# DLRM interaction tower on one core: ScalarE's copies of the first half's gram no longer stand behind the weight transfers

## The reference

```python
e = jnp.stack([tbl_0[ids[:, 0]], ..., tbl_26[ids[:, 26]]], axis=1)      # (2048, 27, 128)
interactions = jnp.einsum('bfd,bgd->bfg', e, e).reshape(B, F * F)
z = jnp.concatenate([r_bottom_mlp_out, interactions[:, TRIL_IDX]], axis=1)
h = jnp.concatenate([z, r_bottom_mlp_out], axis=1)                        # (2048, 607)
h = jnp.maximum(h @ W_top1 + b_top1, 0.0)                                 # 512
h = jnp.maximum(h @ W_top2 + b_top2, 0.0)                                 # 256
y = h @ W_top3                                                            # 1
```

## Time and profile before

| | |
|---|---|
| plain runs, median of 3 | 412.73 us (412.5 to 413.49) |
| profiled execution, span from first to last instruction | 563.8 us |
| mean granted TensorE clock in it | 0.845 |
| TensorE busy | 395.0 us (70% of the span) |
| POOL busy | 292.0 us (52%) |
| VectorE busy | 231.8 us (41%) |
| ScalarE busy | 156.7 us (28%) |
| DMA, mean | 72 GB/s |

### The profile page before, as it was taken

How to read it: one execution, slowest core, us unless ns; L and a number is a source line. 1 busy time by engine, 2 the same in 40 slices (tenths; PEclk the granted TensorE clock), 3 DMA queues, 4 the chain that set the end, 5 groups by cost and what they waited for, 6 DMA issues and landing times.

```text
span 563.8 us, 9147 instructions
## 1 busy us (share of the span) xinstructions
PE 395.0 (70%) x3669; PEld 336.8 (60%) x3669; DVE 231.8 (41%) x430; ACT 156.7 (28%) x337; POOL 292.0 (52%) x284
## 2 busy tenths in 40 slices
PE   1620868397979578688939587797979490924987
PEld 1520756285868467576737376676857390823977
DVE  3530667073836143373617052472716050422430
ACT  3200543021424142324115042322215041401433
POOL 6776007656574747374735737373746656172010
PEclk9975898688989979699969879697979785885999
DMA  8761272122331312041411212140413111030000
GB/s 212 193 170 47 79 185 70 48 84 66 93 86 29 99 35 74 23 118 34 145 28 62 76 33 72 24 117 24 131 37 75 48 53 51 6 95 19 16 8 9
DMA packets 20737, 40.50 MB, mean 72 GB/s; under 512 B 7128, under 2 KB 11428, under 8 KB 20696
## 3 DMA queue, kind: packets, MB, share of 16 engines
q1 hardware_dynamic: 11674, 21.64, 14.1%
q0 software_dynamic: 8960, 18.22, 12.8%
q10 hardware_dynamic: 62, 0.06, 0.1%
HBM read 36.81 MB, written 0.01 MB: 65 GB/s over the span
## 4 chain that ended last, share of the span: by engine, by line
PE 51%; issue 18%; another core or an unknown queue 11%; DVE 8%; DVEq 3%; ACT 3%; DMA 3%; SPq 1%; ACTq 0%
PE col_bank L687 17%; PE gram_bank L723 15%; PE mlp_bank L778 6%; PE mlp_bank L746 6%; DVE mask L583 4%; PE col_bank L706 4%; DVEq L590 3%; PE mlp_bank L742 2%; DMA b<-in_b 2%; DVE mask L587 2%; ACT eT L438 1%; DMA pairs<-in_tbl 1%; DVE parts L624 1%; DVE eT L608 1%
## 5 line engine op out<-in xcount | busy, mean ns | idle before, releaser
L311 POOL DMA_INDIRECT rows<-in_tbl,idx x272 | 285.5, 1050 | 219.2 <-PE gram_bank L723 138.1
L687 PE MATMUL col_bank<-mask,parts 125*128 125x512 f32 (+3 forms) x768 | 168.0, 381 | 21.8 <-DVE parts L624 12.2
L687 PEld LDWEIGHTS col_bank<-mask,parts 125*128 125x128 f32 x768 | 139.8, 204 | 45.0 <-DVE parts L624 12.1
L583 DVE TENSOR_SCALAR mask<-hot_i,rowid 125x1024 fp32r<-125x1024 int32 (+3 forms) x152 | 103.9, 684 | 65.0 <-remote 30.6
L723 PE MATMUL gram_bank<-eT 128*58 128x52 f32 x2048 | 87.2, 244 | 59.6 <-issue 54.0
L723 PEld LDWEIGHTS gram_bank<-eT 128*58 128x58 f32 x2048 | 78.5, 160 | 71.3 <-issue 67.1
L618 DVE COPY pairs<-gram_bank 26x208 f32<-26x208 f32 x128 | 46.7, 365 | 159.4 <-remote 91.5
L706 PE MATMUL col_bank<-ident,rows 128*128 128x128 f32 x272 | 41.7, 293 | 82.5 <-issue 30.5
L468 ACT ACTIVATE pairs<-gram_bank 26x208 f32<-26x208 f32 x128 | 44.5, 348 | 153.0 <-remote 84.6
L706 PEld LDWEIGHTS col_bank<-ident,rows 128*128 128x128 f32 x272 | 32.4, 149 | 90.7 <-issue 88.4
L424 ACT ACTIVATE eH<-col_bank 128x512 f32<-128x512 f32 (+3 forms) x30 | 15.3, 516 | 148.4 <-issue 59.6
(11 more groups left out here) (34 smaller groups left out, 83.9 us busy)
## 6 DMA issues: line engine op xcount, KB each, us to landing
hot_i<-in_hot_ids SPq DMA_DIRECT2D x13, 512.0 KB
rows<-in_tbl,idx POOLq DMA_INDIRECT x272
pairs<-in_tbl SPq DMA_DIRECT2D x8, 448.0 KB
hot_i<-in_hot_ids SPq DMA_DIRECT2D x8, 256.0 KB
pairs<-in_tbl SPq DMA_DIRECT2D x2, 560.0 KB
bottom<-in_bottom SPq DMA_DIRECT2D x8, 128.0 KB
hot_i<-in_hot_ids SPq DMA_DIRECT2D x2, 384.0 KB
x<-pairs SPq DMA_DIRECT2D x16, 39.0 KB
```

The lines of the kernel that those rows point to most:

```text
L311: pool.indirect_dma_start(out=rows_of(h, g)[:, i * D:(i + 1) * D], out_offset=None, in_=tables[GATHERED_TABLES[f]], in_offset=bass.Indirec ...
L583: last = nc.vector.tensor_scalar(mask[0:ROWS, entry % MASKS, 0:2 * size], ids, row_of(ks[0], c), None, ALU.is_equal)
L687: last = nc.tensor.matmul(col_bank[fill % BANKS][:, 0:size], parts[k][0:ROWS, part, c * D:(c + 1) * D], mask[0:ROWS, entry % MASKS, at:at ...
```

## The change

ScalarE's wait for the nine weight transfers, between placing half 0 in `eT` and copying half 0's gram, is left out. Nothing is put elsewhere; VectorE's and TensorE's own waits for the weights stay.

```diff
@@ -516,7 +516,6 @@
                         act.wait_ge(col_copied[fill % BANKS], fill // BANKS + 1)
                 last = place_hot(0, m)
             last.then_inc(hot_copied, 1)
-            act.wait_ge(weights_loaded, 16 * WEIGHT_LOADS)
 
             copy_pairs(0)
             place_early(1)
```

## The result

The changed kernel takes 411.67 us (median of 20 runs) where the kernel before takes 412.81 (20 runs): ratio 0.9965, with a 95% interval of 0.9949 to 0.9981. So it is faster by 1.4 to 2.4 us, and not by the 5.2 us that were forecast.

A forecast was written before the change was run, and what follows sets the result against it. It took a plain run as mostly TensorE's work, with TensorE or POOL the bound later. Stop 3.3 + set 0.9 + lookup 2.0 = 6.2 us, or 4.2 if POOL; middle 5.2, so 407.5 us, range 404.0 to 412.8.

The forecast's parts named there:

- The wait and the stop: Half 0's gram: without ScalarE's 5.44 us wait for the last bias, TensorE no longer stops before the fourth set, 3.27 us less.
- the upper bound: Front of a plain run: gathers beside the weights put them back by about 2.4 us, so the gain could reach 8.6 us.
- The clock: TensorE behind the stop: full clock returns 0.9 us in the fourth gram set and 2.0 us in the lookup.
- The rule taken from the Trainium skill: TensorE: after waiting long enough for a transfer it is throttled and restarts at half rate; with it 6.2 us, without 3.3.
- VectorE's masks: Lookup behind half 0's gram: masks at 0.765 us each keep up with TensorE's 0.94 us per entry.
- a sign of being wrong: Half 0 or 1: the forecast is wrong if TensorE stops at another place for as long.
- All three come 4.2 us earlier: End of half 0's fourth gram set: SyncE's x transfers, POOL's half 2 gathers and TensorE's lookup start 4.2 us earlier.
- Either may be: Halves behind half 0's gram: TensorE or POOL may be the bound, gaining up to 6.2 or 4.2 us; middle 5.2 taken.
- A: Half 0's gram: in a plain run the weights are in time and ScalarE never waits; 412.7 us, no change; chance 0.11.
- B: Half 1's copies: x stands in line behind the weights, so asking 4.2 us earlier brings nothing; 412.7 us; chance 0.04.
- C: Half 1's copies: x lands late beside weights and ids, TensorE stops at the fourth set; 417.9 us; chance 0.05.
- The 10.35 us of the earlier trace: Half 1's copies: their wait until 108.81 us in the profile ahead of the prediction, used for B and to price C.

The follow-up runs named there:

- base_d: The kernel before, unchanged, run again for an undisturbed profile; 413.69 us beside 413.14, ratio 0.9983.
- few_wait_c: The kernel before, with the wait, without 3 of the 17 gathers of each half from half 2 on; 395.89 us, ratio 0.9564.
- delay16_b: The changed kernel with 16 unneeded copies on ScalarE where the wait stood; ratio 1.0034 to the kernel before.
- delay32: The changed kernel with 32 unneeded copies on ScalarE where the wait stood; ratio 1.0271 to the kernel before.
- delay8_b: The changed kernel with 5.3 us of unneeded copies on ScalarE where the wait stood, second run; 410.3 us, ratio 0.9918 to the kernel before.
- after_c: The changed kernel itself, run again on one chip with a delayed version; 411.3 us, ratio 0.9941 to the kernel before.
- The doses: The changed kernel with 8, 16 or 32 unneeded copies on ScalarE where the wait stood; ratios 0.9921, 1.0034 and 1.0271 to the kernel before.
- few_nowait_c: The changed kernel without 3 of the 17 gathers of each half from half 2 on; 388.66 us, ratio 0.9399 to the kernel before.
- base_again: The kernel before, unchanged, run again for a second profile at a disturbed time; 551.5 us beside 550.5.
- delay8: The changed kernel with 8 unneeded copies on ScalarE where the wait stood; ratio 0.9921 to the kernel before.

## Why the prediction was wrong

**The wait and the stop.** Right in kind, and low in size: 3.27 us forecast, 4.07 measured in base_d and 5.97 in few_wait_c. The bias landed 18.5 us after the last table's request in base_d and not 16.7. There the gathers run beside the weights, as the upper bound had it with 2.4 us; that they are the reason was not tested.

**The clock.** The fourth set takes 1.06 us in place of 1.40, and the lookup 7.55 in place of 8.77, the very 7.55 of the earlier trace rows. The granted clock in the kernel before (base_d) and in the changed one, stretch by stretch:

```profile
56.00:57.00 1.00, 0.87 (x26) 0.87 (x28) 0.00 (x0) 0.94 (x4) 0.76 (x1) 0.84 0.33 87
57.00:58.00 1.00, 1.00 (x13) 0.86 (x10) 0.41 (x2) 0.93 (x4) 0.18 (x1) 0.50 0.13 33
58.00:62.00 4.00, 4.00 (x15) 3.16 (x14) 3.50 (x6) 1.76 (x4) 3.09 (x2) 0.74 0.19 47
```

```profile
52.00:54.00 2.00, 2.00 (x10) 1.64 (x9) 1.89 (x4) 1.61 (x4) 1.73 (x1) 1.00 0.76 216
54.00:58.00 4.00, 4.00 (x20) 3.30 (x19) 3.27 (x5) 0.00 (x0) 3.08 (x4) 1.00 0.40 119
...
62.00:66.00 4.00, 3.44 (x15) 3.06 (x15) 2.56 (x5) 1.93 (x4) 3.08 (x4) 0.50 0.21 60
```

So 0.3 + 1.2 us came back where 0.9 + 2.0 were forecast: the clock fell later, inside the set, and was back sooner. The rule taken from the Trainium skill ("TensorE: Matmul & The Clock Gate", HAM oscillation) agrees with this pair: with the stop of 4.07 us the clock is at 1.2 GHz behind it, without it at 2.4. How much it costs differs: behind the stops of 5.97 to 18.78 us in few_wait_c, delay16_b and delay32 the set took 1.84 or 1.85 us, but behind 2.92 us in delay8_b it took 1.06, at full clock.

**VectorE's masks.** Here the working compared rates, 0.765 us for a mask against 0.94 us of TensorE per entry, and found cover. It should have counted: VectorE makes 10 masks between the fourth set's copies and its copy of lookup 4. Those 10 take from 58.24 to 67.0 in base_d, and from 52.44 to 61.4 in the changed kernel, 9 us in both. TensorE's faster lookup (7.55 us) so ends in a wait of 3.13 us for VectorE's copy, where it was 1.35. Counted from the start of the gram in each, that copy comes at 67.19 - 49.29 = 17.9 and 61.52 - 47.28 = 14.2 us, a lead of 3.7 us; the 1.2 us of clock in the lookup were given back at once.

The prediction named as a sign of being wrong that TensorE stops at another place in half 0 or 1 for as long. This is that place: 3.13 us in the changed kernel's profile and 2.72 in after_c. In the first of them the clock fell behind it (0.50 in 62 to 66, above), and half 1's gram took 4.51 us, where it took this in base_d:

```profile
70.92 3.62 PE L723 MATMUL gram_bank<-eT 128*58 128x52 f32 x128 [0.63 <-DVE eT L608]
```

Counted from the start of half 0's gram, half 1's gram ends 25.3 us later in base_d and 23.7 in the changed kernel: 1.6 us of lead are left. In after_c half 1's gram took 3.62 us and the lead was 4.1. Since the two are equally far from the forecast time, this is not what held the gain down.

**POOL: the step that failed.** "All three come 4.2 us earlier", said of SyncE, POOL and the lookup, was wrong for POOL. It rested on POOL's 31.79 us of waiting. That wait belongs to the disturbed execution, in which TensorE came to the gram at 76 us and POOL was through with its gathers at 53.4. In an undisturbed one the gram begins at 47 to 49 us and POOL is busy with half 1 until 57.2. The prediction had the two halves of this in hand: it estimated the weights' request at 42 us (37 was measured), and put POOL's gathers beside the weights in the upper bound. It did not ask the same question of POOL's own release. With its numbers, the gram of the kernel before would have ended at 42 + 19.3 = 61 us and POOL at 53.4, still a wait. With the measured ones, 36.9 + 20.6 = 57.5 for the gram and 57.2 for POOL, it was over in 1.14 us, of which 0.8 could be won and no more. The doses and the table above show it in the wait's place: without the wait for the gram POOL is kept by its own gathers.

**Which engine is the bound.** "Either may be" was right as a statement, and taking the middle of 4.2 and 6.2 was the error that came of the step above. For POOL the gain is that of its wait, and this was 0.8 us, for TensorE 6.4. few_wait_c and few_nowait_c show the second, the doses the first. The medians gained 1.4 and 2.4 us, 0.6 to 1.6 more than POOL's wait, and where that comes from is open. The last gathers are issued at 382.26 in base_d and 381.49 in after_c, 0.8 us apart with equal busy times of POOL; in the changed kernel's first profile they end at 378.58, but there POOL was busy for 2.9 us less, by chance as far as these runs tell. After the last gather base_d takes 29.4 us and the four profiles without a wait on POOL 27.5 to 28.3, but delay16_b, with one, takes 27.6.

**The rivals.** A: refuted, ScalarE waits over 6 us. B and C: half 1's copies do not wait for x at all. In the changed kernel they start 2.15 us after ScalarE fell idle, released by TensorE:

```profile
66.43 4.51 PE L722 MATMUL gram_bank<-eT 128*58 128x52 f32 x128 [0.63 <-DVE eT L607]
...
68.37 0.69 ACT L468 ACTIVATE pairs<-gram_bank 26x208 f32<-26x208 f32 x2 [2.15 <-PE gram_bank L722]
```

The 10.35 us of the earlier trace rows were of the disturbed execution too. The forecast of the direction came true. The measured gain is below the forecast's own range of 3.3 to 8.6 us, and the time lies in the full range only because that was stretched to take in A and B, which are both wrong. That is luck: it lies there because of a mechanism that none of the rivals had: a second engine, behind in its own work, on which the removed wait weighed only with its last 0.8 us.

## What to carry to other kernels

A wait on the chain is worth, once removed, only what it holds up on the engine that has the least slack. So follow each of its successors and ask when that engine would be ready by its own work; for one with a fixed backlog (here 38 gathers on POOL) this is a sum that takes a minute. When the profiled execution is a third longer than the plain runs, its order of events is suspect as well, although it was taken here as safe to read: redo the arrival times of every engine for the shorter front before using a wait from it. And of two engines in step, compare how many instructions each has in the stage, not how long one of them takes.

## What was unexpected of the hardware

The same program takes 412 us at one time and 530 to 570 at another. It is not the chip: the one that gave 544.8 us for the kernel before also gave 414.12. In the long executions TensorE stands still with nothing to wait for that the profile shows. Here are its gram's weight loads and matmuls in base_again, the matmuls alone with 65.2 us in 79 pieces, and then the weight loads in the changed kernel's short execution:

```profile
PEld gram_bank L723 <- issue: 79.0, 96, 3.2
...
PE gram_bank L723 <- issue: 65.2, 79, 2.8
```

```profile
PEld gram_bank L722 <- issue: 7.6, 16, 1.9
```

POOL's and ScalarE's busy times hardly differ between the two (298.9 against 296.8 us and 156.9 against 156.4 in base_again and base_d). TensorE's grow from 358.5 to 395.1, at a lower clock of 0.869 against 0.963. What causes this was not found; the runs only show that it changes which engine is the bound.

A stop of the same length does not always cost the same clock. In delay8 and delay8_b TensorE stops for 2.92 us before the fourth set; the set then took 1.85 us in the one and 1.06 in the other. TensorE's next stops, for VectorE's copy behind the lookup, were 3.13 us in the changed kernel and 3.25 in few_nowait_c; half 1's gram then took 4.51 and 3.62 us.
